# A graph network on one core: 3224 tiles of edges in place of 3232, and a scatter whose slot bound sits in one register

## The reference

```python
h = jnp.maximum(_layernorm(x, axis=-1), 0.0)
x = x + relu(segment_sum((einsum('nd,rdo->nro', h, W0))[src, type] * weight1, dst))          # layer 0
...
x = x + relu(concat([h, segment_sum(relu(concat([h[src], ea64]) @ M_W.T + M_b), dst)]) @ U_W.T + U_b)   # layer 1
...
x = x + segment_sum(h[src] @ W2[type], dst)                                                  # layer 2
...
msg = h[dst] + (ea16 @ We + be); agg = segment_sum(msg, src)                                 # layer 3
x = x + layernorm(relu(((1 + eps) * h + agg) @ W1 + b1) @ W2l + b2) * gamma + beta
```

## Time and profile before

| | |
|---|---|
| median of three executions | 23065.33 us |
| the profiled execution | 23081.41 us, of it span 23079.6 us |
| POOL busy | 15540.0 us, 67% of the span |
| DVE busy | 10242.7 us, 44% |
| PE busy | 9435.0 us, 41%, at a granted clock of 0.5 nearly throughout |
| g0, g1, g2: first to last gather | 4497.9 to 8533.3, 8738.2 to 12869.2, 13363.6 to 17399.3 us |
| scatter of line 1123, first to last | 17509.2 to 21673.4 us |

### The profile page before, as it was taken

The page is one execution under the profiler, slowest core; times in us unless marked ns, Lnnn a source line. Parts: engine busy times, 40 slices in busy tenths (PEclk is TensorE's granted clock), DMA queues, the critical chain, the costliest instruction groups (busy, mean ns, idle before and its releaser), DMA issues. The chain is left out here.

```text
span 23079.6 us, 208272 instructions
## 1 busy us (share of the span) xinstructions
PE 9435.0 (41%) x48147; PEld 7205.3 (31%) x48150; DVE 10242.7 (44%) x25180; ACT 1861.0 (8%) x4901; POOL 15540.0 (67%) x16453
## 2 busy tenths in 40 slices
PE   0777776433333334333333543333332222222366
PEld 0333333233333333333333333333331111111254
DVE  7777777544444443333333432222224333333473
ACT  5000000000000000000000100000001111111100
POOL 0777777777777767777777267777776777777400
PEclk8555555555555555555555655555555555555686
DMA  2333332222222232222222322222223222222462
GB/s 86 99 98 98 99 98 81 70 64 61 64 61 62 63 45 62 61 63 61 61 61 61 72 89 63 61 64 61 64 61 64 83 83 83 83 82 82 131 222 69
DMA packets 1005113, 1785.47 MB, mean 77 GB/s; under 512 B 352294, under 2 KB 461123, under 8 KB 1004534
## 3 DMA queue, kind: packets, MB, share of 16 engines
q1 hardware_dynamic: 484294, 1127.71, 15.6%
q0 software_dynamic: 513696, 654.80, 12.5%
q10 hardware_dynamic: 7056, 2.21, 0.0%
HBM read 1279.37 MB, written 510.79 MB: 78 GB/s over the span
## 5 line engine op out<-in xcount | busy, mean ns | idle before, releaser
L1018 PE MATMUL psum<-arena 128*128 128x64 f32 x19392 | 4447.2, 424 | 7925.5 <-DMA arena<-table,arena 4589.6
L919 POOL DMA_INDIRECT arena<-table,arena x6464 | 6104.2, 944 | 2005.8 <-issue 1932.5
L1018 PEld LDWEIGHTS psum<-arena 128*128 128x128 f32 x19392 | 4226.9, 330 | 8146.0 <-issue 6208.1
L970 DVE TENSOR_TENSOR arena<-arena,psum 128x64 f32 x9696 | 2150.5, 222 | 6333.8 <-PE psum L1018 4413.8
L687 POOL DMA_INDIRECT rec<-arena x3125 | 3001.1, 960 | 1476.0 <-issue 949.0
L1123 POOL DMA_INDIRECT rec<-arena x3232 | 3180.4, 984 | 1093.8 <-issue 971.1
L919 POOL DMA_INDIRECT arena<-ptable,arena x3232 | 3147.6, 974 | 997.8 <-issue 984.3
L464 PE MATMUL psum<-arena 128*128 128x196 bf16 (+1 forms) x4375 | 1378.5, 429 | 1262.4 <-DVE arena L595 1262.3
L1142 DVE TENSOR_TENSOR arena<-psum,arena 128x1024 bf16<-128x1024 f32 x404 | 494.6, 1224 | 2716.2 <-DMA arena<-rec 2716.2
L1190 PE MATMUL psum<-arena 128*128 128x128 bf16 x3232 | 418.0, 311 | 2526.8 <-DVE arena L1142 2526.8
L1190 PEld LDWEIGHTS psum<-arena 128*128 128x128 bf16 x3232 | 312.7, 141 | 2673.6 <-DVE arena L1142 2345.0
(11 more groups left out here) (189 smaller groups left out, 10301.8 us busy)
## 6 DMA issues: line engine op xcount, KB each, us to landing
arena<-rec SPq DMA_DIRECT2D x303, 1408.0 KB
arena<-rec SPq DMA_DIRECT2D x440, 488.0 KB, 4.4
arena<-in_edge SPq DMA_DIRECT2D x625, 232.0 KB, 2.6
arena<-rec SPq DMA_DIRECT2D x404, 352.0 KB, 3.3
arena<-table,arena POOLq DMA_INDIRECT x6464, 2.4
rec<-arena POOLq DMA_INDIRECT x6357, 2.3
table<-arena SPq DMA_DIRECT2D x196, 512.0 KB
arena<-ptable,arena POOLq DMA_INDIRECT x3232, 2.4
```

What stands on the lines that cost most here:

```text
L919: nc.gpsimd.indirect_dma_start(rows[q][:, j * D:(j + 1) * D], None, tab, bass.IndirectOffsetOnAxis(ap=idx[:, j, field:field + 1], axis=0)) ...
L970: v.tensor_tensor(block_sum, block_sum, ps[q % SB][:, j * D:(j + 1) * D], ALU.add).then_inc(s_add[j], 1)
L1018: last = nc.tensor.matmul(ps[q % SB][:, j * D:(j + 1) * D], hot[q % SB][:, j * P:(j + 1) * P], rows[q][:, j * D:(j + 1) * D], start=True, ...
```

## The change

`TILES` is rounded up to a multiple of 8 and no longer of 32: the worst case is 3223 tiles, so `TILES` is 3224 and `GROUPS` is 403. In the gathers `REST` is then 7, which isn't a multiple of `LG` = 4, so SP's last load of records takes 3 groups; in the scatter `REST` is 3. The group that goes is the last one, which holds pads alone. The tables of block numbers (`blkd`) and the records in HBM get shorter by the same 8 tiles, so that every SBUF buffer behind `blkd` starts 32 bytes earlier in its partition, and what lies behind `rec` in HBM moves by 360448 bytes. `QUADS`, `GROUPS2` and all sizes of the second order stay. In the scatter the bound is moved into a register once, ahead of the loop, and each scatter names this register.

```diff
-TILES = -(-((E + NB * (P - 1)) // P) // (G * RING)) * G * RING
+TILES = -(-((E + NB * (P - 1)) // P) // G) * G
...
-                for k in range(groups // LG):
-                    for q in range(k * LG, (k + 1) * LG):
+                for k in range(-(-groups // LG)):
+                    n = min(LG, groups - k * LG)
+                    for q in range(k * LG, k * LG + n):
 
                         wait_earlier(sp, s_g[q], i * (16 * G))
                     wait_earlier(sp, s_sum[q] if relu_q else s_hot[q], i)
-                    sp.dma_start(loads[k].rearrange("p (g w) -> p g w", g=LG), recg[:, bass.ds(i * RG + k * LG, LG), :]).then_inc(s_ld[k], 16)
+                    sp.dma_start(loads[k][:, 0:n * G * RW].rearrange("p (g w) -> p g w", g=n),
+                                 recg[:, bass.ds(i * RG + k * LG, n), :]).then_inc(s_ld[k], 16)
...
+            bound = pool.to_reg(SLOTS2 - 1)
+
...
-                                                     bounds_check=SLOTS2 - 1, oob_is_err=False).then_inc(s_sc[q], 16)
+                                                     bounds_check=bound, oob_is_err=False).then_inc(s_sc[q], 16)
```

## The result

The changed kernel takes 23025.78 us (median of 20 executions, 23012.0 to 23035.91); the kernel before took 23062.43 us beside it (20 executions, 23055.1 to 23086.5). The ratio is 0.9984, with a 95% interval of 0.9977 to 0.999: 36.7 us less, 0.16%. The gain is real and lies within the 0.2% that the prediction called no change. 50.0 us were forecast, and 13 of them are missing.

A forecast was written before the change was run, and what follows sets the result against it. POOL was taken to pace most of the kernel, the landing of the last pad groups to end the gathers. Terms of 39.7 and 10.3 us sum to 50.0, taking 23065.3 to 23015.3 us; range 22975 to 23045 us.

The forecast's parts named there:

- Step 1: Ends of gathers g0, g1, g2: one group of pads less saves its landing, 13.22 + 13.31 + 13.20 = 39.7 us.
- A: Rival for the gathers: pad groups count at POOL's pace, 3 x 10.0 + 10.3 = 40.3 us, 23025 us; chance 0.10.
- The rule by size: Gather DMAs: time follows size, so 32 KB stays under POOL's 1.25 us in every group, pads or not.
- Step 2: Scatter: one group less at POOL's pace, tail behind the last scatter constant; 8 x 1.289 = 10.3 us.
- Step 3: Scatter: 3232 MOVEs become one, hidden because POOL's sequencer runs 12 scatters ahead; 0 us, bounds 0 and 93.7.
- Step 4: First stage: 8 pads less to write, 4.4 us hidden by SP's wait for DVE; 0 us, upper bound 4.4.
- Step 5: Gathers: SP's shorter last load, buffers 32 bytes earlier and tables moved in HBM cost nothing; 0 us.
- B: Rival for the scatter: the MOVEs are on the path, 143.7 us less in all, 22922 us; chance 0.07.
- C: Rival in g1: more gathers held by DVE's add, 0.5 us each, up to 23121 us; chance 0.07.

The follow-up runs named there:

- plus3: The changed kernel with three groups of pads more, 406 groups; 23132.82 us, ratio 1.0042 to the kernel before.
- same_sbuf: The changed kernel with `blkd` keeping room for 3232 words, so the gathers' buffers lie where they lay before; 22989.24 us, ratio 0.9979 to the kernel before.
- spread: The kernel before, with each pad's two row indices its lane's number, so 128 different rows; slow chip, 26987.36 us, ratio 1.0007.
- best_again: The changed kernel with pads of 128 different rows and an SBUF memset ahead of g1's add; 22971.12 us, ratio 0.9968 to the kernel before.
- reg_only: The kernel before with only the scatter's bound moved into a register; 23037.32 us, ratio 1.000.
- tiles_only: The changed kernel with the scatter's bound given as a number again, 3224 tiles; 22998.38 us, ratio 0.9983 to the kernel before.
- before_32: The kernel before with every SBUF buffer behind `blkd` 32 bytes later; slow chip, 26980.02 us, ratio 1.0003.
- before_32_again: The kernel before with every SBUF buffer behind `blkd` 32 bytes later, on a faster chip; 23032.32 us, ratio 0.9993.
- after: The changed kernel itself, with both parts of the change, against the kernel before; 23025.78 us, ratio 0.9984.
- after_spread: The changed kernel with pads of 128 different rows and no memset; slow chip, 26924.58 us, ratio 0.9983 to the kernel before.
- best2: The changed kernel with pads of 128 different rows and a PSUM memset ahead of g1's add; slow chip, 26944.05 us, ratio 0.9991.

## Why the prediction was right or wrong

- **Step 1, 39.7 us for three groups of pads: right.** The last steps are 13 us, PE trails POOL by 3 us less in each gather than before (23.6, 23.5 and 23.7 us against 27.1, 27.2 and 26.1), one group less costs what the landing costs, and `plus3` and `same_sbuf` give 47.9 and 48.8 us for a group where the sum of steps 1 and 2 is 50.0. The guess on the cause, reads of one and the same row, is shown by the packets of `spread` and the steps of `best_again`. The time doesn't show this step by itself: 36.7 us less is nearer to A's 40.3 than to 50.0, and that the changed kernel takes A's 23025 us is chance, two losses that A didn't have either. The rule by size that was weighed there (the Trainium skill, DMA: Bandwidth & Descriptors, section Measured (HBM→SBUF, 128 partitions, SWDGE, issued from GpSimd)) gives, as an estimate, 32 KB under POOL's pace, pads or not; the runs are in line with it for pads with 128 rows (steps of 10.0 us) and against it for pads with one (13.2 to 13.8).
- **Step 2, 10.3 us: right.** 12.7 in the profiled pair, some 2.5 of it the faster execution. The tail behind the last scatter isn't quite constant, as that step had it: from the end of the scatter to the next load 10.2 us with 404 groups, 9.5 with 403 and 11.6 with 406.
- **Step 3, 0 us for the MOVEs: right.** `reg_only` has a ratio of 1.000, and the scatter's 983 ns are the same with and without them.
- **Step 4, 0 us: right for line 224** (its 4.4 us are hidden), but the stage isn't untouched.
- **Step 5, "0 us. ... no row shows a cost of that" for the 32 bytes: this failed.** Line 207's loads take 75 ns more with the buffers moved, 3.9 us of the first stage; this was nowhere in the sum. And g1's held gathers take 10.6 us more. 50.0 - 3.9 - 10.6 = 35.5, against 36.7 measured. That it comes out so well is partly luck, since the two losses are of one pair of executions and the 36.7 of medians; `same_sbuf` against `tiles_only` has 9.1 us for both together. Nor did the buffers all move by 32 bytes, as the section on the change has it: `last` and the pad's record moved by 96.
- **Rival A fell** by the lag's growth in `plus3`, **B** by `reg_only`. **C**, more hits, is in part what happened: 23 more, where it needed 100 to take the gain away. Its price (0.5 us each) was right, and its ground, a phase of tens of ns, is what the table shows. But a gather isn't held "for as long as the rest of the add lasts": in the earlier trace rows that rest is 0.64 us and the hold 0.51, and an add that started 0.56 us or more ahead of a gather holds nothing. The argument held against it, that the executions of before lie within 22 us, was weak: from chip to chip the hits move by 80. Whether they are drawn anew in each execution no run shows; the two traces of one chip and one place (`reg_only`, `same_sbuf`) have 117 both.
- The predicted 23015 us lies 11 us below the median, inside the range; but the chance that the gain stays under 0.2% was given 0.36, though the forecast lay 4 us from that line and the two terms of step 5 were at nothing without a row that showed it.

## What to carry to other kernels

Padding of an indirect gather isn't free by being idle work: 128 indices that all name row 0 cost 13 to 14 us for 8 gathers where 128 different rows cost POOL's 10, and it is a matter of two instructions to give pads different rows. Where POOL set the pace that took 68.6 us of lag out of three stages; leaving a group out gave 37 to 49. Read the end of a stage apart from its middle: the engine that leads the page wasn't what ended these stages. And a change that shifts buffers by some bytes should be compared with one that keeps them in place (a spare allocation, for each table that shrinks), or its small gain is mixed with the move. And where the same kernel is slower on another chip, look in its trace for what sets the pace there before a run on it is read.

## What the runs showed of the hardware

- With 128 indices of one row, a DMA packet of an indirect gather takes 414 to 595 ns in the mean (`before_32`, `before_32_again`), and 64 to 65 with 128 different rows (`spread`, `best_again`).
- A load of a register from SBUF (line 207) takes 0.62 us on SP and 0.65 on ACT, and 0.70 and 0.72 in `after` and `tiles_only`, where the buffers lie 32 bytes earlier and the words read 96; with the buffers 32 and 64 bytes later it is as fast as before. It isn't the address of the word, since the same addresses are read by fast loads and by slow ones. Why is open.
- DVE's add of two SBUF tiles holds an indirect gather if it starts 0.046 us or more ahead of it, and then until 0.81 to 0.83 us behind the add's own end; at 0.043 us or less it doesn't at all (the seven traces of the table; in those of the slow chips without a memset the least that holds is 0.036). The Trainium skill, SBUF — State Buffer, section Who interferes with whom, has the first issuer block the other, which fits. That a memset ahead of the add, even one that writes PSUM, leaves the gather held though the add starts 0.2 us behind it fits it less: by that section a DVE instruction with at most one SBUF input, outside the 2-port modes, doesn't contend, so the memset should hold nothing. These runs don't tell which of the two begins the hold.
- An instruction that loads the scatter's bound into a register (MOVE, 29 ns) costs nothing ahead of an indirect scatter: one comes each 1.2881 us with it (`tiles_only`) and without it (`reg_only`).
- The chips aren't alike: the kernel before took 23038 to 23062 us in three of the comparisons and 26971 in two others. In the latter PE's matmuls in the gathers have some 2500 gaps of 1 to 3.5 us with nothing seen to wait for, 5.7 to 5.8 ms in all, and the faster chips have none, while a DMA packet in the middle of g0 takes as long as elsewhere (85 ns in `before_32`, 90 in `before_32_again`). What holds PE there is open, and all that hangs on POOL's pace (this change too) is worth something else on such a chip: `after_spread`, with less to gather and different rows, gained 47 us there, `best2` 28.
